# Rope halves of an attention loop exchanged on VectorE instead of by a second query product

## What is computed

```python
q = (x @ Wqa @ Wqb)                     # 64 latent columns -> 16 heads x (128 nope + 64 rope)
k_nope, v = split((compressed @ Wkvb))  # compressed and k_pe from x @ Wkva
q_pe, k_pe = rope(q_pe), rope(k_pe)     # o1 = x1*cos - x2*sin ; o2 = x1*sin + x2*cos
scores = einsum([q_nope, q_pe], [k_nope, k_pe]) / sqrt(192), causal
out = softmax(scores) @ v, then @ Wout
```

## Time and profile before

| what | before |
|---|---|
| median of 3 runs (lowest, highest) | 1889.39 us (1889.11, 1890.69) |
| the profiled execution | 1887.92 us |
| its span | 1885.9 us |
| mean granted TensorE clock | 0.97 |
| busy over the span | PE 93%, PEld 76%, DVE 62%, ACT 52%, POOL 31% |

### The profile page before, as it was taken

The page is one execution under the profiler, slowest core; times in us unless marked ns, Lnnn a source line. Parts: engine busy times, 40 slices in busy tenths (PEclk is TensorE's granted clock), DMA queues, the critical chain, the costliest instruction groups (busy, mean ns, idle before and its releaser), DMA issues. The chain is left out here.

```text
span 1885.9 us, 32569 instructions
## 1 busy us (share of the span) xinstructions
PE 1760.9 (93%) x11524; PEld 1436.0 (76%) x11524; DVE 1170.7 (62%) x2801; ACT 971.8 (52%) x2291; POOL 581.0 (31%) x482
## 2 busy tenths in 40 slices
PE   4758999999999999999999999998599999999998
PEld 3536777777877877877777787786488888888887
DVE  3526777777777777777777777674544454454543
ACT  2425666666666666666666666664233333333332
POOL 5334343343443434434344343441001100110100
PEclk8758999999999999999999999999799999999999
DMA  8030000001200000200000100000400000000000
GB/s 234 34 138 24 17 9 10 18 9 35 77 9 10 18 9 23 79 18 10 10 18 23 40 18 9 10 1 12 141 1 23 16 8 24 23 1 23 12 12 12
DMA packets 39852, 57.49 MB, mean 30 GB/s; under 512 B 4624, under 2 KB 32592, under 8 KB 39184
## 3 DMA queue, kind: packets, MB, share of 16 engines
q1 hardware_dynamic: 39696, 55.42, 9.3%
HBM read 40.21 MB, written 15.20 MB: 29 GB/s over the span
## 5 line engine op out<-in xcount | busy, mean ns | idle before, releaser
L816 ACT ACTIVATE probs<-aps,nmax 128x256 f32<-128x256 f32 (+7 forms) x512 | 378.1, 740 | 272.0 <-DVE nmax L858 259.7
L858 DVE CUSTOM_DVE_ANT_0 aps<-aps,mask_row 128x256 f32<-128x256 f32 (+7 forms) x512 | 387.4, 768 | 191.4 <-PE aps L42 181.0
L756 PE MATMUL aps<-ident,probs 128*128 128x128 f32 x2304 | 323.2, 274 | 0.5 <-DVE pT L881 0.3
L42 PE MATMUL aps<-kTh,qh 128*128 128x512 f32 (+3 forms) x768 | 290.1, 378 | 8.2 <-ACT probs L816 5.3
L756 PEld LDWEIGHTS aps<-ident,probs 128*128 128x128 f32 x2304 | 265.6, 140 | 33.5 <-issue 7.1
L42 PE MATMUL aps<-pT,v 128*64 128x512 f32 (+3 forms) x1536 | 268.9, 492 | 0.8 <-DVE pT L881 0.8
L42 PE MATMUL aps<-kTl,qh 128*128 128x512 f32 (+3 forms) x768 | 257.4, 343 | 0.0
L827 ACT COPY pT<-aps 128x512 f32<-128x512 f32 (+3 forms) x448 | 207.1, 477 | 54.2 <-PE aps L756 49.8
L42 PE MATMUL aps<-kTh,ql 128*128 128x512 f32 (+3 forms) x768 | 221.9, 343 | 0.0
L42 PEld LDWEIGHTS aps<-pT,v 128*64 128x64 f32 x1536 | 102.1, 136 | 153.1 <-issue 142.8
L926 POOL TENSOR_TENSOR rot<-rot 64x512 f32<-64x512 f32 x128 | 163.8, 1280 | 169.8 <-DVE rot L871 169.6
(11 more groups left out here) (180 smaller groups left out, 3141.0 us busy)
## 6 DMA issues: line engine op xcount, KB each, us to landing
wqs<-wq_scratch SPq DMA_DIRECT2D x32, 384.0 KB, 3.1
xb<-in_x SPq DMA_DIRECT2D x4, 1024.0 KB, 8.8
acc<-in_x SPq DMA_DIRECT2D x8, 512.0 KB, 3.7
x_scratch<-acc SPq DMA_DIRECT2D x8, 512.0 KB, 2.9
x<-x_scratch SPq DMA_DIRECT2D x8, 512.0 KB, 3.9
out<-x SPq DMA_DIRECT2D x7, 512.0 KB, 3.0
wq_scratch<-wq_all SPq DMA_DIRECT2D x8, 384.0 KB, 5.0
keys_scratch<-stage SPq DMA_DIRECT2D x2, 1536.0 KB, 5.1
```

Source lines behind the costliest of these rows:

```text
L42: return nc.tensor.matmul(out, lhsT, rhs, start=start, stop=stop, skip_group_check=True)
L756: last = nc.tensor.transpose(tps[:, TS.index(x) % 3, j * P:(j + 1) * P], probs[c][:, c * (pair % 2), a, off:off + P], t.ident[:])
L816: nc.scalar.activation(probs[c][:, c * (r % 2), a, off:off + w], sps[:, at:at + w], ACT.Exp, bias=nmax[:, c, a, j:j + 1], scale=-1.0, accu ...
L858: nc.vector.tensor_tensor_reduce(out=s, in0=s, in1=mask[:, N - PW[c][j]:N], scale=-1.0, scalar=3.0e38, op0=ALU.add, op1=ALU.min, accum_out ...
```

## The change

The swapped columns of the query weights are gone: `wq_all` and the scratch in HBM have 256 columns instead of 384, so each `load_wq` moves 256 KB instead of 384 KB. `Q(c, 0)` makes two matmuls instead of four and takes one bank. `ROT` reads the plain product twice more: two passes of 32 partitions, one from partitions 32 to 63 to rows 0 to 31, one from 0 to 31 to rows 32 to 63. All four tables and the bank table are new, and the wait of `load_wq` takes the later of the two Q(1, a).

```diff
@@ weights and their columns
-        wq = sb("wq_all", [P, PAIRS, 2, 3 * P], F32R)
+        wq = sb("wq_all", [P, PAIRS, 2, 2 * P], F32R)
...
                 cols.append((a, slice(P * a + 32 * k, P * a + 32 * k + 32), k))
-                cols.append((a, slice(2 * P + 64 * a + 32 * k, 2 * P + 64 * a + 32 * k + 32), 1 - k))
@@ load_wq
-                    sp.wait_ge(q_ps, count(Q(1, 1), r - 1))
+                    sp.wait_ge(q_ps, max(count(Q(1, a), r - 1) for a in range(2)))
@@ q_job
-                    outs = [(BANK[x], a * P)] + ([(SWAPPED[c], 2 * P)] if a == 0 else [])
-                    for bank, col in outs:
-                        for wp in range(2):
-                            last = mm(nc, banks[:, bank, :], wqs[:, pair % 2, wp, col:col + P], rhs, wp == 0, wp == 1)
+                    for wp in range(2):
+                        last = mm(nc, banks[:, BANK[x], :], wqs[:, pair % 2, wp, a * P:(a + 1) * P], rhs, wp == 0, wp == 1)
@@ rot_job
-                    nc.vector.tensor_tensor(rot2[:, k, :], sps[64 * a:64 * a + 64, swapped:swapped + QC],
-                                            t.sinT[:, cols], ALU.mult).then_inc(q_rot, 1)
+                    for to, source in ((0, 32), (32, 0)):
+                        last = nc.vector.tensor_tensor(rot2[to:to + 32, k, :], sps[source:source + 32, at:at + QC],
+                                                       t.sinT[to:to + 32, cols], ALU.mult)
+                    last.then_inc(q_rot, 1)
@@ the tables (one line of each end)
-        TENSOR = [T(1, 2, 0), S(0, 0, 2), S(0, 0, 3), T(1, 3, 1), S(0, 1, 3), T(1, 1, 1), Q(1, 0), T(1, 1, 0),
+        TENSOR = [T(1, 1, 0), T(1, 3, 1), S(0, 1, 0), S(0, 0, 0), S(0, 1, 2), T(1, 0, 1), S(0, 0, 2), Q(1, 1),
```

More of the change, by code:

```diff
@@ L450, in sem @@
             return ctx.enter_context(nc.semaphore(name))
-        wqs = sb("wqs", [P, 2, 2, 3 * P], F32R)
+        wqs = sb("wqs", [P, 2, 2, 2 * P], F32R)
         qh, ql = sb("qh", [P, 2, N], F32R), sb("ql", [P, 2, N], F32R)
@@ L545, in ACC @@
             return ("acc", c, i)
-        TENSOR = [T(1, 2, 0), S(0, 0, 2), S(0, 0, 3), T(1, 3, 1), S(0, 1, 3), T(1, 1, 1), Q(1, 0), T(1, 1, 0),
[L549 to L572, removed]
+        TENSOR = [T(1, 1, 0), T(1, 3, 1), S(0, 1, 0), S(0, 0, 0), S(0, 1, 2), T(1, 0, 1), S(0, 0, 2), Q(1, 1),
+                  T(1, 3, 0), L(1), T(1, 2, 0), Y(0, 0), T(1, 1, 1), S(0, 0, 1), T(1, 2, 1), S(0, 1, 1),
+                  S(0, 1, 3), T(1, 0, 0), S(0, 0, 3), T(1, 7, 0), T(1, 4, 0), Q(1, 0), Q(0, 1), PV(1, 0, 4),
+                  S(1, 1, 2), T(1, 7, 1), T(1, 6, 0), T(1, 5, 1), Q(0, 0), L(0), T(1, 4, 1), T(1, 5, 0),
+                  T(1, 6, 1), S(1, 0, 3), S(1, 0, 0), T(0, 1, 0), PV(1, 4, 4), S(1, 1, 0), T(0, 0, 1),
+                  S(1, 0, 2), T(0, 0, 0), T(0, 1, 1), S(1, 0, 1), T(0, 3, 1), T(0, 2, 0), T(0, 3, 0), Y(0, 1),
+                  Y(1, 0), T(0, 2, 1), S(1, 1, 1), S(1, 1, 3), PV(0, 0, 4), Y(1, 1)]
@@ new lines, in attention @@
+        VECTOR = [INV(1), MAX(0, 1, 0), MAX(0, 0, 0), MAX(0, 1, 2), MAX(0, 0, 2), ROT(1, 1), ACC(0, 0),
+                  OUT(1, 1, 1), MAX(0, 0, 1), MAX(0, 1, 1), MAX(0, 1, 3), MAX(0, 0, 3), ROT(1, 0), INV(0),
+                  ROT(0, 1), MAX(1, 1, 2), ROT(0, 0), OUT(1, 5, 0), OUT(1, 6, 1), MAX(1, 0, 3), MAX(1, 0, 0),
+                  OUT(0, 1, 0), O(1), MAX(1, 1, 0), OUT(0, 0, 1), MAX(1, 0, 2), OUT(0, 1, 1), MAX(1, 0, 1),
+                  OUT(0, 2, 0), OUT(0, 3, 0), ACC(0, 1), ACC(1, 0), OUT(0, 2, 1), MAX(1, 1, 1), MAX(1, 1, 3),
+                  O(0), ACC(1, 1)]
@@ new lines, in attention @@
+        SCALAR = [OUT(1, 1, 0), OUT(1, 3, 1), EXP(0, 1, 0), EXP(0, 0, 0), OUT(1, 0, 1), EXP(0, 1, 2),
+                  EXP(0, 0, 2), OUT(1, 3, 0), LOUT(1), OUT(1, 2, 0), OUT(1, 2, 1), HIGH(1, 1), EXP(0, 0, 1),
+                  EXP(0, 1, 1), OUT(1, 0, 0), EXP(0, 1, 3), EXP(0, 0, 3), OUT(1, 7, 0), OUT(1, 4, 0),
+                  HIGH(1, 0), OUT(1, 7, 1), OUT(1, 6, 0), OUT(1, 5, 1), EXP(1, 1, 2), HIGH(0, 1), LOUT(0),
+                  OUT(1, 4, 1), EXP(1, 0, 3), HIGH(0, 0), EXP(1, 0, 0), OHIGH(1), EXP(1, 1, 0), OUT(0, 0, 0),
+                  EXP(1, 0, 2), OUT(0, 3, 1), EXP(1, 0, 1), EXP(1, 1, 1), EXP(1, 1, 3), OHIGH(0)]
@@ new lines, in attention @@
+        POOL = [REP(1), ADD(1, 1), LOW(1, 1), ADD(1, 0), REP(0), LOW(1, 0), ADD(0, 1), LOW(0, 1), ADD(0, 0),
+                LOW(0, 0), OLOW(1), OLOW(0)]
+        BANK = {S(0, 1, 0): 1, S(0, 0, 0): 2, S(0, 1, 2): 3, S(0, 0, 2): 0, Q(1, 1): 1, L(1): 2, Y(0, 0): 3,
+                S(0, 0, 1): 0, S(0, 1, 1): 1, S(0, 1, 3): 2, S(0, 0, 3): 3, Q(1, 0): 0, Q(0, 1): 1,
+                S(1, 1, 2): 2, Q(0, 0): 0, L(0): 1, S(1, 0, 3): 2, S(1, 0, 0): 0, S(1, 1, 0): 2, S(1, 0, 2): 0,
+                S(1, 0, 1): 2, Y(0, 1): 0, Y(1, 0): 1, S(1, 1, 1): 2, S(1, 1, 3): 0, Y(1, 1): 2}
@@ L617, in slot @@
             return 512 * BANK[x]
-        SWAPPED = {c: BANK[Q(c, 0)] + 1 for c in range(NC2)}
         def banks_of(x):
-            return (BANK[x], BANK[x] + 1) if x in (Q(0, 0), Q(1, 0)) or (x[0] == "s" and x[1] == 1) else (BANK[x],)
+            return (BANK[x], BANK[x] + 1) if x[0] == "s" and x[1] == 1 else (BANK[x],)
         def bank_users(x, r):
@@ L633, in bank_users @@
                     if exists(y, rr):
-                        users.add((Q(y[1], 1) if y[0] == "q" and bank == SWAPPED[y[1]] and y[2] == 0 else y, rr))
+                        users.add((y, rr))
                         break
@@ L864, in rot_job @@
                     cols = slice(c * QC, (c + 1) * QC)
-                    at, swapped, k = slot(Q(c, a)), 512 * SWAPPED[c], QS.index(Q(c, a)) % 2
+                    at, k = slot(Q(c, a)), QS.index(Q(c, a)) % 2
                     n = count(Q(c, a), r)
@@ L1613, in build @@
         t = Shared()
-        t.wq_dram = nc.dram_tensor("wq_scratch", [PAIRS, P, 2, 3 * P], F32, kind="Internal").ap()
+        t.wq_dram = nc.dram_tensor("wq_scratch", [PAIRS, P, 2, 2 * P], F32, kind="Internal").ap()
         t.kq_dram = nc.dram_tensor("keys_scratch", [2, P, 3, N], F32, kind="Internal").ap()
```

## The result

The changed kernel takes 1900.71 us (median, 1899.00 to 1900.88), the kernel before, run beside it, 1889.25: a ratio of 1.0059, 95% interval 1.0042 to 1.0076. It is slower by 0.6%. The prediction was 1876 us, faster, with a range that ended at 1890: the sign is wrong, and the time is outside the range.

What follows compares the result with a forecast made beforehand. PE, busy without gaps, was taken as the bound: -19.2 us over 31 bodies, +7.6 at sequence ends, -0.4 for the first load, sum -12.0 from 1887.92; forecast 1876 us, range 1856 to 1890.

Steps and rivals of the forecast that it cites:

- What leaves PE: In each body, two query products lose two matmuls each, 0.23 us a matmul: -0.92 us a body.
- The mixing: PE's switching between kinds of jobs in a body gets cheaper: -0.15 us, ends -0.4 and +0.2.
- The pass of 32 partitions: In the rotation on DVE, each new pass takes 0.69 us, with ends 0.60 and 1.4.
- DVE's share: In the loop, DVE goes from 26.2 to 28.4 us a body, 80% of 35.5, without becoming the bound.
- The wait at `Y(0,1)`: PE waits for the bank that S(1,0,2) frees late, after MAX and EXP: +0.45 us a body.
- The same sum for `S(1,1,2)` and `S(1,0,3)`: Bank wait of PE between these two score tiles: 0 to 0.2 us a body, taken as 0.
- All other bank pairs: Elsewhere in the body, banks come free in time for PE with 0.2 us or more to spare.
- the ends of the sequences: At r = 8 and 16 PE waits for late query weights, 2.5 us twice, plus clock loss: together +7.6 us.
- The clock: Behind each sequence-end gap PE may run at 0.50, losing 2.6 us; at an even chance +1.3 us each.
- The start of the loop: Body 0 loses about 0.9 us of matmuls and gains as much waiting: 0; the smaller first load gives -0.4 us.
- given back at the ends and in the bodies: Gaps of 3 us, longer clock falls, one more 0.3 us wait a body: about 1890 us, chance 0.11.
- VectorE takes over: ROT(0,0) delays MAX(1,0,3), with passes of 1.4 us: 2 us a body, 1940 us, or 1909 at half price; chance 0.11.

Runs made afterwards that it cites:

- the last run above: Changed kernel with the next pair's query weights requested ahead of sequence-end stores and loads, plus S(1,0,2) moved ahead of T(0,0,1): 1883.93 us, ratio 0.9973 to the kernel before.
- the run with the early weights: Changed kernel with the next pair's query weights requested ahead of the sequence's stores and loads, not behind them: 1886.07 us, ratio 0.9984 to the kernel before.
- The runs with one pass: Changed kernel, query weights requested earlier, sine step one pass of 64 partitions instead of two of 32: 1880.6 us with two query matmuls, 1902.3 with four.

## Why the prediction was wrong

- **What leaves PE**, -0.92 us a body: right. The runs with doubled matmuls give +0.93 for the two blocks.
- **The mixing**, -0.15 (-0.4 to +0.2): within its ends, and half the size. With both waits taken out, 35.96 - 36.13 + 0.92 - 0.53 - 0.29 leaves -0.07.
- **The pass of 32 partitions**, 0.69: right; the 256 passes show 681 ns. **DVE's share**, 28.4 us a body, 80%: right, 79%.
- **The wait at `Y(0,1)`**, +0.45: right in place and cause, 0.53 measured. The 2.16 us of PE's work are right; the way is 2.69 instead of 2.61, since PE starts 0.14 us behind the end of EXP and I had given it 0.06.
- **The first step that failed**: "The same sum for `S(1,1,2)` and `S(1,0,3)` gives 0 to 0.2 ...: I take 0." It is 0.29 us in every body, 9 us in all. As printed, the count is wrong: 14 transposes and a query product make 1.91 us and would leave 0.64. PE has 15 transposes there and four more of `L(0)`, 2.46 us measured, and against 2.55 that does lie within 0 to 0.2. What fails is the way itself: 2.75 us instead of 2.55, with 0.15 from EXP's end to PE, which I left out here though its neighbour got 0.06 for it, and 0.05 more ahead of EXP. "All other bank pairs came out with 0.2 us or more to spare" does not hold either: between `S(1,0,1)` and `S(1,1,1)` PE has 2.00 us of work and the way takes 2.45, so this pair is in time only because PE waits at `Y(0,1)` in between, as the last run above shows. A body: -0.92 - 0.07 + 0.53 + 0.29 = -0.17 instead of -0.62; over the loop that is 14.1 us of the miss of 24.7.
- **The second**: the ends of the sequences, +7.6, measured +15.1, confirmed by the run with the early weights. The sum's store left in time, but SP's next issue came 4.76 us later, 1.9 more than in the kernel before (2.90), and the weights landed 7.3 us after issue: 14.5 us behind the store, where I had 10.8 to 12.3 from the kernel before. The low end of that was a misreading: in the kernel before, the load that the product needs, issued at 474.00, took 7.0 us; the 5.5 belong to the one issued behind it at 476.5. PE came 10.1 us into the body, near the 9.7 worked out. At the second end the store took 2.95 us and the landing 7.4. Idle 5.28 and 3.55 instead of 2.5 twice. The clock: I took half of 2.6 us; it fell to 0.50, the 1.2 GHz level, both times, for 5.4 us and 4.0 us at the least, and the bodies lost 3.2 and 3.05 us besides the idle time. Half a chance on a gap of this length was too kind. By the prediction's working the product needed these weights 9.6 us earlier in its body than before (9.7 instead of 19.3); that was the whole of the cost, and one reordered load was the cure.
- **The start of the loop**: 0 taken for body 0 and -0.4 for the first load, +1.8 measured, of which +3.7 from the first query product to body 2 and -1.9 by chance ahead of it. The 0.4 cannot be told from that chance. Body 0 has idle times of 4.72 and 2.31 us before the low parts of the query on POOL are there, against 2.05 and 0.62 in the kernel before and 1.53 for a rotation. I let the longer rotation chain and the saved matmuls cancel there. The runs with one pass take 3.5 and 4.6 us of it away again, so it is the price of the longer chain.
- **Behind the loop**, nothing taken, +0.9. No run tests this part.

Of the rivals the third, "given back at the ends and in the bodies", was the mechanism, with its terms still too small: it had one more wait of 0.3 us a body, which is right, and 14 us at the ends, right too, but left out the start and gave the bodies -0.32 where they got -0.17. (Its own sum, +4, stands above 1889 and so gives 1893, not 1890.) The second, "VectorE takes over", is refuted for this kernel: 100 us of VectorE's work taken away gave 5.5 us, 3.5 of them ahead of body 2 and 2 in the bodies. Its place, `MAX(1,0,3)` behind `ROT(0,0)`, shows no wait. With the old order the rival would have come true, without its price of 1.4 us a pass: passes of 0.69 add 1.4 us of waits to a body there. So the new order is what makes the exchange on VectorE bearable, and it has a price of its own: with one pass it is 9 to 13 us slower than the old one (1880.6 against 1871.2 with two matmuls, 1902.3 against 1889 with four).

The rule of the Trainium skill ("Perfetto Trace Analysis", section "Identifying the Most-Contended Engine") pointed at weight loads and, through them, at VectorE. (The section names a second measure for TensorE beside weight loads, MFU, the share of the peak arithmetic; it was not worked out here.) The rows decide against it here: PE's weight loads were busy 76%, VectorE 80%, and it was four matmuls more on PE that moved the body (0.64 us), not four passes fewer on VectorE (0.07).

## What to carry to other kernels

When an engine without gaps gets less work, look for the round trips that its work was covering: each bank (or buffer) that goes to another engine and back sets a least distance between two jobs, and a matmul taken out from between them is worth only what is left above that distance. Work added to an engine at 80% can cost 4 us or 50, depending on which banks and whose inputs stand behind it; read this from the lists and the table of banks, not from shares. And when a consumer moves up in the program, follow the queue that feeds it: here 15 us hung on a load that stood behind a store and five other loads.
